# Embedding rows in a one-core language-model layer: one-hot products against a table in SBUF, or row fetches from DRAM by GpSimd

## What is computed

```python
t = jnp.minimum(tokens, 63)
feat_emb = jnp.concatenate([color_W[t // 16], shape_W[t % 16 // 4], quantity_W[t % 4]], axis=-1)
spec_emb = special_W[jnp.clip(tokens - 64, 0, special_W.shape[0] - 1)]
emb = jnp.where((tokens < 64)[..., None], feat_emb, spec_emb)
out = emb * sqrt(192) + pe[None, :, :]          # pe: sines and cosines of the position
```

## Time and profile before

| | us |
|---|---|
| median of 3 runs | 827.14 |
| lowest and highest of them | 824.53 and 827.54 |
| the profiled execution, device time | 824.91 |
| its span in the profile | 822.8 |
| busy in the span: PE / DVE / ACT / POOL | 769.2 / 646.3 / 547.0 / 287.8 |
| granted TensorE clock, mean | 0.988 of full speed |

### The profile page before, as it was taken

How to read it: one execution, slowest core, us unless ns; L and a number is a source line. 1 busy time by engine, 2 the same in 40 slices (tenths; PEclk the granted TensorE clock), 3 DMA queues, 4 the chain that set the end, 5 groups by cost and what they waited for, 6 DMA issues and landing times.

```text
span 822.8 us, 23184 instructions
## 1 busy us (share of the span) xinstructions
PE 769.2 (93%) x7374; PEld 652.7 (79%) x7374; DVE 646.3 (79%) x1712; ACT 547.0 (66%) x1225; POOL 287.8 (35%) x429
## 2 busy tenths in 40 slices
PE   3658999999999999999999999999999999999897
PEld 2535787888888788888878888887888888787786
DVE  5776987878878788887878888787888778786745
ACT  4836576767767676776767677676767767675533
POOL 3752242343424234342323334232333423242222
PEclk9888999999999999999999999999999999999999
DMA  7500000000000000000000000000000000000000
GB/s 251 197 2 15 2 7 20 8 18 0 23 0 6 18 6 18 0 23 0 6 18 6 18 0 23 0 11 12 6 18 0 23 0 15 8 6 11 2 2 20
DMA packets 17075, 16.77 MB, mean 20 GB/s; under 512 B 6290, under 2 KB 15384, under 8 KB 16792
## 3 DMA queue, kind: packets, MB, share of 16 engines
q1 hardware_dynamic: 17048, 16.43, 6.4%
HBM read 12.23 MB, written 4.19 MB: 20 GB/s over the span
## 4 chain that ended last, share of the span: by engine, by line
PE 86%; DVE 6%; issue 3%; ACT 2%; POOL 1%; DMA 1%; SPq 0%; DVEq 0%; POOLq 0%; ACTq 0%
PE bank L1518 38%; PE bank L1904 11%; PE bank L1831 7%; PE bank L1690 6%; PE bank L1679 5%; PE bank L1800 4%; PE bank L1787 3%; PE bank L1778 3%; PE bank L1764 2%; DVE xa L1102 2%; ACT er L752 1%; PE bank L1619 1%; PE bank L1546 1%; DVE mr L1159 1%; PE bank L1624 1%
## 5 line engine op out<-in xcount | busy, mean ns | idle before, releaser
L1159 DVE SCALAR_TENSOR_TENSOR mr<-er,gm 128x512 f32<-128x512 f32 x192 | 126.7, 695 | 6.5 <-ACT er L752 4.7
L752 ACT ACTIVATE er<-bank 128x512 f32<-128x512 f32 x192 | 106.1, 596 | 24.8 <-PE bank L1679 24.6
L1904 PE MATMUL bank<-w2t,w_raw 128*128 128x192 f32 x576 | 112.4, 326 | 0.0
L1102 DVE SCALAR_TENSOR_TENSOR xa<-xr,cw_,xa 128x256 f32<-128x256 f32 x192 | 93.0, 493 | 7.2 <-ACT xa L672 5.6
L836 ACT ACTIVATE sg<-bank 128x256 f32<-128x256 f32 x144 | 55.2, 383 | 61.5 <-PE bank L1518 52.7
L1904 PEld LDWEIGHTS bank<-w2t,w_raw 128*128 128x128 f32 x576 | 91.0, 190 | 1.1
L1518 PE MATMUL bank<-x_h,wt_lo 128*128 128x256 f16 x288 | 78.5, 273 | 0.0
L1518 PE MATMUL bank<-x_h,w_lo 128*128 128x256 f16 x288 | 78.5, 273 | 0.0
L1518 PE MATMUL bank<-x_l,w_hi 128*128 128x256 f16 x288 | 78.5, 272 | 0.0
L1518 PE MATMUL bank<-x_h,wt_hi 128*128 128x256 f16 x288 | 78.4, 272 | 0.0
L1518 PE MATMUL bank<-x_h,w_hi 128*128 128x256 f16 x288 | 78.4, 272 | 0.0
(11 more groups left out here) (243 smaller groups left out, 2153.0 us busy)
## 6 DMA issues: line engine op xcount, KB each, us to landing
out<-w_raw SPq DMA_DIRECT2D x16, 192.0 KB, 2.0
w_raw<-weights SPq DMA_DIRECT2D x1, 1924.0 KB, 9.6
wt_raw<-weights SPq DMA_DIRECT2D x1, 1924.0 KB, 13.6
pos<-position SPq DMA_DIRECT2D x16, 96.0 KB, 2.7
ri<-exponent_rows SPq DMA_DIRECT2D x4, 384.0 KB, 4.4
tok<-tokens SPq DMA_DIRECT2D x16, 70.0 KB
sums<-lj SPq DMA_DIRECT2D x16, 64.0 KB, 2.2
ri<-sums SPq DMA_DIRECT2D x64, 12.0 KB
```

Of the source, the lines that this page charges most:

```text
L752: act.activation(er[:, r % NER], p_d[r % 2][:].rearrange("p (h i) -> p h i", h=HG), ACT.Exp)\
L1102: ve.scalar_tensor_tensor(xa[:, m], xr[:, m, :, k:k + Q], cw_[:, m, k:k + 1], xa[:, m], ALU.mult, ALU.add)\
L1159: ve.scalar_tensor_tensor(mr[:, r % NMR], er[:, r % NER], 1.0, gm[:, r // NQ, :].unsqueeze(1).to_broadcast([128, HG, Q]), ALU.min, ALU.mult)\
L1904: ins = pe.matmul(p_ex[e][:, b * D:(b + 1) * D], hh[:, e % NHH, b * Q:(b + 1) * Q], w2t[:, e, :], start=True, stop=True)
```

## The change

The table stays in DRAM, in float32. SP now copies the tokens as one column for each sequence (128 partitions by 2 numbers, from a transposed token array). GpSimd clamps them to the row numbers `row` in one small instruction and issues two indirect transfers, one for each sequence, each of which fetches 128 rows of 768 bytes into `emb`. DVE's `pre_add` scales `emb` and adds the position, reading SBUF in both inputs. The bf16 table and its five setup instructions, the one-hot instruction and the six products of each chunk are gone, and so are the loads of `ids` and of the table. In a body GpSimd does `embed(p)` right after `mixed(b)`, ahead of its wait for `vl_turned`; in the ramp `embed(0)` comes first and `embed(1)` after `keep(0)`.

```diff
@@ SP, load(c)
                 if later(c):
-                    sp.wait_ge(onehot_ready, c)
+                    sp.wait_ge(row_ready, c)
                 settle(sp)
-                sp.dma_start(tok[:], tokens[:, bass.ds(c * Q, Q)].partition_broadcast(V)).then_inc(tokens_in, 16)
+                sp.dma_start(tok[:], tokens[bass.ds(c * Q, Q), :]).then_inc(tokens_in, 16)
...
-            sp.dma_start(ids[:], vocab_ids).then_inc(in_first, 16)
-            sp.dma_start(tab[:], table).then_inc(in_first, 16)
             load(0)
@@ GpSimd
+            def embed(c):
+                pool.wait_ge(tokens_in, c * 16 + 16)
+                if later(c):
+                    pool.wait_ge(emb_in, c * 32)
+                settle(pool)
+                pool.tensor_scalar(row[:], tok[:], float(V - 1), 0.0, ALU.min, ALU.max).then_inc(row_ready, 1)
+                pool.wait_ge(row_ready, c + 1)
+                if later(c):
+                    pool.wait_ge(h0_ready, c)
+                settle(pool)
+                for b in range(NB):
+                    pool.indirect_dma_start(emb[:, b, :], None, table, bass.IndirectOffsetOnAxis(row[:, b:b + 1], 0))\
+                        .then_inc(emb_in, 16)
...
             def ramp():
+                embed(0)
                 keep(0)
+                embed(1)
                 pre(0)
                 pre(1)
...
                 mixed(b)
+                if p is not None:
+                    embed(p)
                 if f is not None:
                     pool.wait_ge(vl_turned, b + 1)
                     decayed(f, 0)
@@ DVE
-            def pre_onehot(c):
...
-            def pre_add(c, src=p_misc):
-                ve.wait_ge(emb_done, c + 1)
+            def pre_add(c):
+                ve.wait_ge(emb_in, c * 32 + 32)
                 ve.wait_ge(position_in, c * 16 + 16)
                 if later(c):
                     ve.wait_ge(h0_copied, c)
-                ve.tensor_tensor(h0_next[:], src[:, 0:NB * D].rearrange("p (b d) -> p b d", b=NB),
-                                 pos[:].unsqueeze(1).to_broadcast([128, NB, D]), ALU.add).then_inc(h0_ready, 1)
+                ve.scalar_tensor_tensor(h0_next[:], emb[:], EMB_SCALE, pos[:].unsqueeze(1).to_broadcast([128, NB, D]),
+                                        ALU.mult, ALU.add).then_inc(h0_ready, 1)
@@ PE
-            def pre_embed(c, dst=p_misc):
...
                     mlp_gate_up(c, f, p_pair[f % 2])
-                    if f == 1 and p is not None:
-                        pre_embed(p)
@@ PE, ramp
-                pe.wait_ge(in_first, 48)
-                pre_embed(0)
+                pe.wait_ge(in_first, 16)
                 pre_turn(0, p_misc, p_pair[1][:, 0:NB * Q])
-                pre_embed(1, p_out[0])
```

More of the change, by code:

```diff
@@ L28 @@
 I32 = mybir.dt.int32
+U32 = mybir.dt.uint32
 NB = 2
@@ L99, in reached, with program @@
         return c * self.per + self.n
-def program(nc, tokens, position, vocab_ids, table, weights, norms, conv_w, conv_b, shared_rows, d_skip, w_out, w_down,
+def program(nc, tokens, position, table, weights, norms, conv_w, conv_b, shared_rows, d_skip, w_out, w_down,
             w2, identity, lower_ones, triangle_rows, exponent_rows, pair_rows, spread_rows, out):
@@ L145, in program @@
         mhalf = sb("mhalf", [128, 2])
-        tok = sb("tok", [V, NB, Q], I32)
+        tok = sb("tok", [128, NB], I32)
+        row = sb("row", [128, NB], U32)
+        emb = sb("emb", [128, NB, D])
         pos = sb("pos", [128, D])
-        onehot = sb("onehot", [V, NB, Q], BF16)
         h0_next = sb("h0_next", [128, NB, D])
@@ L261, in program @@
         tokens_in, position_in = sem("tokens_in"), sem("position_in")
-        onehot_ready, emb_done, h0_ready, stat_ready, r0_ready = (sem(n) for n in (
-            "onehot_ready", "emb_done", "h0_ready", "stat_ready", "r0_ready"))
+        row_ready, emb_in, h0_ready, stat_ready, r0_ready = (sem(n) for n in (
+            "row_ready", "emb_in", "h0_ready", "stat_ready", "r0_ready"))
         uc_ready, uh_ready, ul_ready, uh_turned, ul_turned, u_hi_ready, u_lo_ready = (sem(n) for n in (
@@ L628, in _ @@
         def _(act):
-            act.wait_ge(in_first, 48)
+            act.wait_ge(in_first, 16)
             act.copy(id16[:], idf[:]).then_inc(setup_a, 1)
@@ L1045, in low_in @@
                 ve.tensor_copy(lo[:], src).then_inc(ready, 1)
-            def pre_onehot(c):
-                ve.wait_ge(tokens_in, c * 16 + 16)
-                if later(c):
-                    ve.wait_ge(emb_done, c)
-                ve.tensor_scalar(onehot[:], tok[:], float(V - 1), ids[:, 0:1], ALU.min, ALU.is_equal)\
-                    .then_inc(onehot_ready, 1)
-            def pre_add(c, src=p_misc):
-                ve.wait_ge(emb_done, c + 1)
+            def pre_add(c):
+                ve.wait_ge(emb_in, c * 32 + 32)
                 ve.wait_ge(position_in, c * 16 + 16)
@@ L1433, in ramp @@
                 setup_table()
-                pre_onehot(0)
                 pre_add(0)
                 pre_stats(0)
-                pre_onehot(1)
                 setup_first()
@@ L1441, in ramp @@
                 pre_split(0, p_pair[1][:, 0:NB * Q])
-                pre_add(1, p_out[0])
+                pre_add(1)
                 ve.wait_ge(in_small, 16 * N_SMALL)
@@ L1488, in body @@
                     scanned(f, 0)
-                if p is not None:
-                    pre_onehot(p)
                 swiglu(b, p, f)
@@ L1534, in turn @@
                 ins.then_inc(low_turned, 1)
-            def pre_embed(c, dst=p_misc):
-                if not later(c):
-                    pe.wait_ge(setup_v, SETUP_V)
-                pe.wait_ge(onehot_ready, c + 1)
-                if later(c) and dst is p_misc:
-                    pe.wait_ge(s_ready[0], c)
-                settle(pe)
-                for b in range(NB):
-                    for k in range(3):
-                        ins = pe.matmul(dst[:, b * D:(b + 1) * D], onehot[:, b, :], tab3[:, k, :],
-                                        start=(k == 0), stop=(k == 2))
-                ins.then_inc(emb_done, 1)
             def pre_turn(c, dst=p_misc, low=p_out[1][:, NB * Q:2 * NB * Q]):
@@ L1552, in pre_turn @@
                     pe.wait_ge(setup_a, 1)
+                    pe.wait_ge(setup_v, SETUP_V)
+                elif dst is p_misc:
+                    pe.wait_ge(s_ready[0], c)
                 turn(c, dst, low, u_t, uh_ready, ul_ready, uh_turned, ul_turned)
@@ L2094 @@
 N_ROWS = 2 * NB + 1
-SETUP_V = 9
+SETUP_V = 4
 SETUP_P = 7
@@ L2144 @@
     arrays = {
-        "tokens": x, "position": position, "vocab_ids": np.arange(V, dtype=f32)[:, None],
+        "tokens": np.transpose(x), "position": position,
         "table": np.concatenate([features, L0_tok_special_W], axis=0),
```

15 lines of the change are left out of this document (removed).

## The result

| | before | after |
|---|---|---|
| median of the runs | 827.01 us (824.53 to 827.54) | 851.22 us (849.75 to 852.3) |
| profiled execution, device time | 824.9 us | 849.75 us |
| span | 822.8 us | 847.9 us |
| busy in the span: PE / DVE / ACT / POOL | 769.2 / 646.3 / 547.0 / 287.8 us | 765.6 / 647.2 / 546.7 / 327.6 us |
| granted TensorE clock, mean | 0.988 | 0.987 |

The ratio is 1.0298, with a 95% interval of 1.0272 to 1.0324: slower, by 24.2 us, where about 8 were forecast. The range (825 to 851) ends 0.2 us short of it. The sign was right and so was half of the mechanism of the loop; two terms of the sum were too small, and one was missing.

The account below looks back on a forecast made before the run. PE looked busiest, but DVE's order from 418.6 to 422.5 was taken to set the pace as much. 13 x 0.65 + 0.5 = +8.9 us gave 833.8 from the profiled 824.9 or 836 by the median; forecast 834.5, range 825 to 851.

Parts of the forecast that it names:

- PE's products lie in a hole, gain 0: Six embedding products ahead of tile 2, 0.50 us on the chain: removal gains 0.00 to 0.05 us, taken as 0.
- `pre_add` +0.04, one-hot 0: DVE in a loop body: `pre_add` with two SBUF inputs costs 0.04 us more, removing the one-hot gains 0; both left out.
- GpSimd's `embed`, the term that decides: GpSimd between `rm` and `state`: landing 2.2, clamp 0.42, two transfers 2.2 us; free at 416.39, loss 0.65 a body.
- The estimate by the Trainium skill's figure: Loop alternative, about 1 us to a GpSimd transfer's first byte: free at 416.2, loss 0.45 a body, 5.8 us in all.
- Mask 5 holds the transfers up: Rival of dearer transfers in a loop body: the mask delays them 0.68 us, in all +17.8 us, 843; chance 0.20.
- How a late GpSimd becomes a late PE: Loop body: late `state` delays `y` and the gate, which delays mask 6 and `gt` of tile 2; PE loses 0.65 us.
- The first body outside the ramp, 0: Body ahead of the loop: its tokens arrive much earlier, their transfer being issued in the ramp; no loss counted.
- The ramp, +0.5: Ramp: `r` 1.8 us later behind `embed(1)`, up to 1.25 given back, PE's second six products gone; +0.5 us taken.
- Rows arrive in time in a loop body: Second fetch lands by 419.1, DVE reaches `pre_add` at 419.90 + 0.66; over 1 us to spare.
- The signs: Loop body: transfers end 4.5 to 5.5 us after token issue, `state` about 1 us later, mask 6 delayed, PE waits at tiles 2, 4.
- The sum: Whole run: 13 loop bodies at 0.65 us plus 0.5 for the ramp, +8.9 us; forecast set at 834.5.

Follow-up runs that it names:

- the last one: Changed kernel with rows fetched a body ahead, second fetch early, an exponential earlier, and the third chunk's fetch moved ahead of the ramp's second gate: 819.16 us, ratio 0.9905.

## Why the prediction was wrong in size, point by point

- **PE's products lie in a hole, gain 0.** Right: a body with two of them is 47.85, one with twelve 48.30, and after the change PE waits at tile 2.
- **`pre_add` +0.04, one-hot 0.** Right; `pre_add` took 0.55.
- **GpSimd's `embed`, the term that decides.** This is the step that failed. I had GpSimd free at 416.39; it was free at 417.51 on the same scale, 1.12 later. By its parts: from the tokens' issue to the clamp's start pass 1.99 us, of which the landing is 1.7, where I had 2.2 (0.21 less), and they were issued 0.09 later. From the clamp's start to the first transfer pass 1.07 us, not 0.42 (0.65 more): I counted the clamp and its wait, and no time for the transfer's own start. The two transfers take 2.79, not 2.2 (0.59 more): the first alone is 1.11 and the second 0.97, close to my 1.1, but 0.30 lies between them and mask 5 holds the first one for 0.37 (1.48 against 1.11). The prices of the instructions were good; what stands around an instruction of a new kind (start, distance, port) was left at zero. So the loss of a loop body, forecast as 0.65, came to 1.54. The estimate by the Trainium skill's figure (DMA: Bandwidth & Descriptors, "Specifications"), 5.8 us in all, was further off still.
- **Mask 5 holds the transfers up.** I had this as a rival, +0.68 us and 843, with "it may or may not apply". It applies, with 0.37, and only if the mask starts first. At my own times it would not have: I had the first transfer at 414.19, 0.36 ahead of the mask (414.55), and in the kernel without the clamp a lead of 0.09 to 0.17 us was enough for neither to be held up. The late start of the transfer (414.72 on that scale, the mask at 414.54) brought it in, so the rival's price and its condition were both off.
- **How a late GpSimd becomes a late PE.** Half right: the gate does hold mask 6, for 0.66. By the rule of the prediction (the loss is the moment GpSimd is free, less 415.75) 417.51 would cost 1.76; measured were 1.54 to 1.58, since mask 6 ended 0.55 us after the gate, not 0.69. I had written that `y` ends ahead of 418.63 and so doesn't hold `gt` of tile 0. With the later `state` it does, for 0.88 of the 1.54.
- **The first body outside the ramp, 0.** The fetch there costs nothing, as the run with the early second fetch shows. But body 0 grew by 1.5 us through the clock, a term that the sum didn't have.
- **The ramp, +0.5.** Wrong: +4.3. I followed `r`, which ended 1.8 us late, as the upper end had it (`w_lo` was over, and `r` took 0.72); about 1.7 of the 4.3 are its part. I didn't follow the second fetch's landing, for which I had taken 2.7 everywhere; issued at 13.09 it took 8.12, and DVE waited for it in order, ahead of `dx`.
- **Rows arrive in time in a loop body.** Right; no wait there.
- **The signs.** Mask 6 longer beside the gate, and PE's waits at tiles 2 and 4, came as named, but larger: `state` 2.20 us late against about 1, PE's wait at tile 2 1.54 against about 0.5, and the transfers ended 5.82 us after the tokens' issue against 4.5 to 5.5.
- **The sum.** 13 x 0.65 + 0.5 = 8.9 against 19.3 + 4.3 + 1.5 = 25.1. Of the 16.2 missing, 10.9 are the transfers' starts and the port in the loop, 5.3 the ramp and its clock.

## What to carry to other kernels

Ask of an engine that takes on new work not whether it has idle time but what the next engine waits for behind it: the same two transfers cost 1.54 us a body ahead of `state` and nothing behind `pre(p)`. Before counting a removed instruction as a gain, look whether its place is a hole that another chain holds open; here the gain came only when that chain was shortened as well, 0.00 and 0.04 alone, 0.42 together. The same small fetch landed after 3.07 us at one place of the ramp and after 8.12 at another: do not carry a landing time from one place to another, and try the small loads first, which here won 7.2 us of span together with the earlier `r` and the clock.

## What the runs showed of the hardware

- An indirect transfer of 128 rows, not held up, occupies GpSimd in a loop body for 1.10 to 1.12 us as the first of a pair (or alone) and 0.95 to 0.97 as the second, with 0.30 us between the two. Ahead of the first stand 0.84 to 0.97 us behind the clamp, and about 1.0 behind the tokens' landing when there is no clamp; but only 0.27 behind the clamp at 7.86 in the run with the early second fetch (written there without the semaphore instruction of `settle` in between, so the place is not the only difference), and 0.20 behind `rm` in body 0 of the kernel without the clamp. What makes up this start was not settled; the clamp's hand-over is excluded as the whole of it.
- A mask of DVE with two SBUF inputs, started first, holds an indirect transfer of GpSimd up: the transfer ends 0.98 to 1.00 us after the mask, and 0.03 us ahead is enough. Started second, neither is longer than alone (1.10 and 0.68 in the kernel without the clamp); where both started within 0.02 us in the kernel with one fetch, the transfer was not held and the mask took 0.72 to 0.74.
- The same fetch of rows landed 3.07 us after its issue at 6.39 and 8.12 us after its issue at 13.09, with bulk loads of SP under way beside both (169 GB/s beside the first, 363 to 417 beside the second). The run with the early second fetch shows that the wait goes with the place, not that the fuller DMA engines are its cause: nothing else was varied.
- In seven of the twelve kernels (the changed one, one fetch, gate behind `h_next`, no clamp, twelve products, the earlier exponential, the last one) PE was granted 0.50 to 0.52 for the first 3 us of body 0's scan products, after a wait in which it had little to do; in the other five it was granted 1.00 there, after a similar wait. Body 0 takes 52.42 to 53.81 us in the seven and 50.75 to 51.34 in the five. It cost 1.5 us in the changed kernel, and body 0 of the kernel with the earlier exponential was 53.36 us long instead of 51.34, although it began 0.9 us sooner. A few us more or less in the ramp thus shift the end by more, or less, than themselves.
- In body 0 of each of the three kernels with the rows a body ahead the two transfers took 2.93 or 2.94 and 1.82 us instead of 1.11 and 0.97. They held nobody up, and no run was made for their cause.
